# The running state of a scan mixer formed and kept transposed, and turned back once a tile

## The reference

```
alpha = exp(dt_t * A_neg);  beta = (1 - lam_t) * dt_t * alpha;  gamma = lam_t * dt_t
Bx_t  = u_t[:, :, :, None] * Bp_t[:, :, None, :]
h     = alpha * h + beta * Bx_prev + gamma * Bx_t
y_t   = einsum('bhpn,bhn->bhp', h, Cp_t)
```

## Time and profile before

| | |
|---|---|
| median of 3 runs | 4490.3 us (4488.98 to 4494.2) |
| the profiled execution: its time, its span | 4485.84 us, 4484.1 us |
| third stage in the trace | about 240 to 3266 us |
| TensorE (PE) busy over the span | 4197.9 us, 94% |
| VectorE, ScalarE, GpSimd busy | 3222.6 us (72%), 2157.4 us (48%), 2376.0 us (53%) |

### The profile page before, as it was taken

How to read it: one execution, slowest core, us unless ns; L and a number is a source line. 1 busy time by engine, 2 the same in 40 slices (tenths; PEclk the granted TensorE clock), 3 DMA queues, 4 the chain that set the end, 5 groups by cost and what they waited for, 6 DMA issues and landing times. The chain is left out here.

```text
span 4484.1 us, 118726 instructions
## 1 busy us (share of the span) xinstructions
PE 4197.9 (94%) x39924; PEld 3488.0 (78%) x39924; DVE 3222.6 (72%) x6737; ACT 2157.4 (48%) x5046; POOL 2376.0 (53%) x3284
## 2 busy tenths in 40 slices
PE   5389999999999999999999999999869999989999
PEld 3178788888888888878788788888648888878888
DVE  8867777777677776777767777677636666668888
ACT  3234444454444444444444444444446666645555
POOL 3276666666676666766666666666400000026666
PEclk9699999999999999999999999999979999989999
DMA  8321111111111111111111111111056666633333
GB/s 276 117 81 30 48 39 39 47 39 48 36 38 50 39 48 36 39 50 39 39 45 39 50 39 36 48 39 46 23 134 180 188 180 183 186 94 105 105 105 96
DMA packets 369774, 347.50 MB, mean 77 GB/s; under 512 B 24953, under 2 KB 343289, under 8 KB 360185
## 3 DMA queue, kind: packets, MB, share of 16 engines
q1 hardware_dynamic: 352380, 323.98, 24.2%
q10 hardware_dynamic: 16896, 16.78, 1.1%
HBM read 232.01 MB, written 108.66 MB: 76 GB/s over the span
## 5 line engine op out<-in xcount | busy, mean ns | idle before, releaser
L721 PE MATMUL bank<-w_bc,xnT 128*128 128x512 f32 x3072 | 804.3, 404 | 11.7 <-POOL xnT L1042 11.7
L924 ACT COPY turned_t<-bank 128x512 f32<-128x512 f32 x512 | 300.3, 587 | 982.4 <-PE bank L744 982.3
L721 PEld LDWEIGHTS bank<-w_bc,xnT 128*128 128x128 f32 x3072 | 556.8, 189 | 144.7 <-issue 34.5
L1455 PE MATMUL p_yc<-sig,toep 64*64 64x256 f32 (+14 forms) x16384 | 538.1, 282 | 13.7 <-issue 10.5
L1455 PEld LDWEIGHTS p_yc<-sig,toep 64*64 64x64 f32 x16384 | 475.1, 132 | 89.7 <-issue 43.5
L1050 POOL TENSOR_TENSOR steps<-upto,par 128x512 fp32r<-128x512 f32 x512 | 536.6, 1068 | 0.0
L1159 DVE TENSOR_TENSOR rot<-bank,par 128x512 f32<-128x512 f32 x512 | 350.1, 684 | 209.6 <-PE bank L721 124.7
L1059 POOL TENSOR_TENSOR turned_b<-rot 128x512 f32<-128x512 f32 x256 | 325.9, 1273 | 197.7 <-DVE rot L1160 197.5
L1604 POOL MEMSET xT<- 128x258 f32 x1 | 0.3, 314 | 684.2 <-POOLq L1349 684.2
L1059 POOL TENSOR_TENSOR turned_c<-rot 128x512 f32<-128x512 f32 x256 | 354.5, 1385 | 1.8 <-DVE rot L1160 1.8
L1160 DVE TENSOR_TENSOR rot<-bank,par 128x512 f32<-128x512 f32 x512 | 346.9, 677 | 0.0
(11 more groups left out here) (264 smaller groups left out, 9671.5 us busy)
## 6 DMA issues: line engine op xcount, KB each, us to landing
toep<-taps_dram SPq DMA_DIRECT2D x256, 260.0 KB, 4.1
el<-el_dram SPq DMA_DIRECT2D x256, 128.0 KB, 3.0
xg<-arg_x SPq DMA_DIRECT2D x32, 512.0 KB, 5.1
xnT_dram<-xt_g ACTq DMA_DIRECT2D x32, 512.0 KB, 5.4
xnT_raw<-xnT_dram SPq DMA_DIRECT2D x128, 128.0 KB, 2.5
x_quad<-arg_x SPq DMA_DIRECT2D x32, 512.0 KB, 3.9
x_dram<-x_quad SPq DMA_DIRECT2D x32, 512.0 KB, 3.7
x0T_dram<-conv SPq DMA_DIRECT2D x32, 512.0 KB, 2.8
```

The source lines that it names most:

```text
L721: last = mm(p_bc[c][:, :], xnT[w.q % 2][p][:, k, :], w_bc[q][:, k, c * 1024 + g * W4:c * 1024 + (g + 1) * W4], start=(n == 0), stop=(n == ...
L924: s_.copy(turned_t[g][c][:, :], p_tr[:, :]).then_inc(s[f"copy_{BC[c]}"], 1)
L1455: last = mm(by_seq(p_y[p][c][odd * H:(odd + 1) * H, 0:2 * TILES])[:, :, first:], toep[n % SLOTS][c * H:(c + 1) * H, lag * H:(lag + 1) * H] ...
```

## The change

The state is kept a second time, in `state_p`, with 64 head columns on partitions: the even heads on partitions 0 to 63, the odd ones on 64 to 127, and for each pair of heads 128 state columns along, again 128 x 512. `new_state` now takes `u_w` of a head as the stationary operand (128 x 64) and B (128 x 128) as the moving one, and writes 64 partitions. `fade_state` and `carry_state` work on `state_p`. A new step of TensorE, `turn_state`, transposes it in four 128 x 128 pieces into the bank of the transposes, and a new step of ScalarE, `copy_state`, copies that to `state`, which `outputs` reads as before. The decay over a tile is the same on all partitions, so that 4 columns of scalars hold what 8 did, one half of the partitions for even and one for odd heads.

```
-P_COS, ... P_EL, P_ET, P_ALL = 0, 8, 24, 40, 48, 56, 64, 72, 80
+P_COS, ... P_EL, P_ET, P_ALL = 0, 8, 24, 40, 48, 56, 64, 72, 76
...
-            s_.activation(col(P_ET), as3(pp[2][:, :]), ACT.Exp)
+            for e in range(2):
+                rows = slice(e * HEAD_U, (e + 1) * HEAD_U)
+                s_.activation(params[rows, :, P_ET:P_ET + HEADS // 2], as3(pp[2][rows, :])[:, :, e::2], ACT.Exp)
...
-    BANK_TR = (..., ("over_b0", "copy_b0", 1, 0))
+    BANK_TR = (..., ("over_b0", "copy_b0", 1, 0), ("turn_state", "copy_state", 1, -1))
...
             def outputs(i, w, g):
-                wait_for(pe, "carry_state", i - 1)
+                wait_for(pe, "copy_state", i - 1)
...
             def new_state(i, w):
                 for h in range(HEADS):
-                    v = slice(h * HEAD_U, (h + 1) * HEAD_U)
-                    last = mm(p_state[:, v], turned(w, h // GROUP, 0)[:, (h % GROUP) * STATE:(h % GROUP + 1) * STATE], u_w[:, v],
-                              start=True, stop=True)
+                    pair, e = h // 2, h % 2
+                    last = mm(p_state[e * 64:(e + 1) * 64, pair * STATE:(pair + 1) * STATE], u_w[:, h * HEAD_U:(h + 1) * HEAD_U],
+                              turned(w, h // GROUP, 0)[:, (h % GROUP) * STATE:(h % GROUP + 1) * STATE], start=True, stop=True)
...
+            def turn_state(i, w):
+                wait_for(pe, "carry_state", i)
+                bank_read(pe, BANK_TR, "turn_state", i + 1)
+                for pair in range(4):
+                    c = slice(pair * 128, (pair + 1) * 128)
+                    last = tp(p_tr[:, c], state_p[1 - w.q % 2][:, c], ident[:, :])
+                last.then_inc(s["turn_state"], 1)
...
                     tile(q, 0, project_u)
+                    tile(q, 1, turn_state)
                     if q == 1:
                         quad(2, widen, 4)
...
+            def copy_state(i, w):
+                wait_for(act, "turn_state", i)
+                wait_for(act, "outputs1", i - 1)
+                s_.copy(state[1 - w.q % 2][:, :], p_tr[:, :]).then_inc(s["copy_state"], 1)
...
                     tile(q, 0, copy_turned, 0, 0)
+                    tile(q, 1, copy_state)
                     if q == 0:
                         quad(2, normalised, 2, 1)
...
             for p in range(2):
                 g_.memset(state[p][:, :], 0.0)
+                g_.memset(state_p[p][:, :], 0.0)
...
             def fade_state(i, w):
                 wait_for(pool, "carry_state", i - 1)
-                wait_for(pool, "outputs1", i - 1)
-                g_.tensor_tensor(all_heads(state[1 - w.q % 2][:, :]), all_heads(state[w.q % 2][:, :]), over(param(P_ET, w), HEAD_U),
+                wait_for(pool, "turn_state", i - 2)
+                g_.tensor_tensor(heads(state_p[1 - w.q % 2][:, :]), heads(state_p[w.q % 2][:, :]), over(par[w.p][:, w.q, P_ET:P_ET + HEADS // 2], STATE),
                                  ALU.mult).then_inc(s["fade"], 1)
...
             def carry_state(i, w):
-                v_.tensor_tensor(state[1 - w.q % 2][:, :], p_state[:, :], state[1 - w.q % 2][:, :], ALU.add)
+                v_.tensor_tensor(state_p[1 - w.q % 2][:, :], p_state[:, :], state_p[1 - w.q % 2][:, :], ALU.add)
```

More of the change, by code:

```diff
@@ L22 @@
 LN_EPS, RMS_EPS = 1e-5, 1e-6
-P_COS, P_SIN, P_A, P_G, P_RHO, P_W, P_EL, P_ET, P_ALL = 0, 8, 24, 40, 48, 56, 64, 72, 80
+P_COS, P_SIN, P_A, P_G, P_RHO, P_W, P_EL, P_ET, P_ALL = 0, 8, 24, 40, 48, 56, 64, 72, 76
 P_EARLY = P_G
@@ L549, in mixer_and_first_ffn @@
     decay, own, mix = two("decay", [128, W4]), two("own", [128, W4]), two("mix", [128, W4])
-    u_g, u_w, state = sb("u_g", [128, 512]), sb("u_w", [128, 512]), two("state", [128, 512])
+    u_g, u_w, state, state_p = sb("u_g", [128, 512]), sb("u_w", [128, 512]), two("state", [128, 512]), two("state_p", [128, 512])
     y_from, yT, el = two("y_from", [128, H64]), two("yT", [128, 512]), two("el", [128, 4, TOK])
@@ L567, in mixer_and_first_ffn @@
     names = ("project_b project_c rotate_b rotate_c turn_b turn_c over_b over_c copy_b copy_c steps logs exp diagonal own gram mix outputs take_y "
-             "values gate_values weigh_values new_state fade carry_state split_hi split_rest sum_over mean_sq square_y pair_sums scan_rstd project_out "
+             "values gate_values weigh_values new_state fade carry_state turn_state copy_state split_hi split_rest sum_over mean_sq square_y pair_sums scan_rstd project_out "
              "residual1 rstd1 norm1 xn_over first_column shifted mixed key relu key_sq receptance tanh value gated residual2 rstd2 norm2 "
@@ L590, in wait_loaded @@
         wait(eng, s[f"{what}{w.p}"], 16 * ((w.n - w.p) // 2 + 1) if isinstance(w.n, int) else 8 * (w.n + (2 - w.p)))
-    BANK_TR = (("over_c1", "copy_c1", 1, -1), ("over_b1", "copy_b1", 1, -1), ("over_c0", "copy_c0", 1, 0), ("over_b0", "copy_b0", 1, 0))
+    BANK_TR = (("over_c1", "copy_c1", 1, -1), ("over_b1", "copy_b1", 1, -1), ("over_c0", "copy_c0", 1, 0), ("over_b0", "copy_b0", 1, 0), ("turn_state", "copy_state", 1, -1))
     BANK_ARG = (("logs0", "exp0", 1, 0), ("new_state", "carry_state", 1, -1), ("logs1", "exp1", 1, 0))
@@ L1193, in carry_state @@
                 wait_for(dve, "new_state", i)
-                v_.tensor_tensor(state[1 - w.q % 2][:, :], p_state[:, :], state[1 - w.q % 2][:, :], ALU.add).then_inc(s["carry_state"], 1)
+                v_.tensor_tensor(state_p[1 - w.q % 2][:, :], p_state[:, :], state_p[1 - w.q % 2][:, :], ALU.add).then_inc(s["carry_state"], 1)
             def moments(which, places, src, by):
```

## The result

The changed kernel takes 4518.7 us (median of 5 runs, 4514.18 to 4520.99), the one before 4490.25 in the same session (4488.98 to 4494.2): 1.006 times as long, interval 1.0045 to 1.0074. It is slower by 28 us, outside my range. The profiled execution took 4520.99 us, its span is 4519.3.

A forecast was written before the change was run, and what follows sets the result against it. TensorE bounds three quarters of the tiles, a chain outside it q = 0. A quad: +0.56 + d - 0.35 - 0.26 = -0.08 us, times 31 -2.5; +1.05 for zeroings; in all -1.4, giving 4489 us, range 4470 to 4505.

The forecast's parts named there:

- q = 0: Tile ending on a chain outside TensorE: TensorE's gain lost, the copy ahead of `xn` costs 0.56 us a quad, plus d.
- TensorE's sum: `new_state` 0.70 us less, `turn_state` 0.35 or 0.44 more; 1.31 us a quad, 41 us; as a rival, whole: 4450, chance 0.11.
- q = 2: Tile where ScalarE is free and the copy lies under `key` 1: TensorE gains 0.26 us.
- q = 3: Tile where TensorE gains 0.35 us, if anyone uses it; the copy makes `split_xnT` and `y_sq` up to 0.25 late.
- q = 1: Tile where TensorE gains 0.35 us and the copy delays four activations about 1 us, costed at nothing.
- the cover: In q = 1, ScalarE's 1.51 us idle ahead of the next `copy_turned` takes up the copy's 1 us delay.
- d: Move of VectorE's full stretch ahead of the carry in q = 0: between -0.35 and +0.25 or +0.4 us, taken as -0.03.
- hurt twice: Rival: late `y_sq` makes `y_sum` overlap `cut_decay`, 0.72 for 0.46 us; a quad loses 0.35; 4502, chance 0.15.
- the first rival: Chain moves up with TensorE as overlap of `steps` and `cut_decay` resolves: d -0.35, a quad gains 0.40; 4479, chance 0.22.
- the rival's 4502: Time in us of the rival where the copy's late `y_sq` also slows `y_sum`; d about +0.4, chance 0.15.
- The missing overlap: Rival: the pair's heads don't overlap, `new_state` stays near 1.73 us; 1.7 us a quad, 4544, chance 0.05.

The follow-up runs named there:

- packed_only: Changed kernel without `turn_state` and `copy_state`, leaving out the part of y from the state before the tile; 4442.1 us, 0.989 of the kernel before.
- late_copy: Changed kernel with `copy_state` moved behind ScalarE's work for the quads, in q = 3 left in place; 4504.3 us, 1.0027 of the kernel before.
- next_tile: Changed kernel with `turn_state` and `copy_state` moved into the next tile, behind `project_bc` and `square_y`; 4488.9 us, 0.9994 of the kernel before.
- lean_before: Kernel before, with one wait for each PSUM bank use, for the use just before; 4442.2 us, 0.989 of the kernel before.
- lean_after: Changed kernel with one wait for each PSUM bank use, for the use just before; 4454.6 us, 0.9915 of the kernel before.
- next_tile_lean: `next_tile` with one wait for each PSUM bank use; 4428.1 us, 0.986 of the kernel before.
- same_waits: Changed kernel, `turn_state` waiting only for the bank use before it and old uses, except the first, not for `copy_state`; 4513.0 us, 1.0046.
- behind_after: Changed kernel with single waits only in `turn_over` 0,1 and `project_out`, the two steps behind `new_state`; 4515.2 us, 1.0053 of the kernel before.
- turn_only: Kernel before, with four transposes of `state` and a copy to an unread tile at the places of the change; 4565.5 us, 1.0163.

## Why the prediction was wrong

The medians over the quads, from one start to the next (`x2n_over` stands at the end of q = 0; us):

```
                  last new_state   to new_   to new_    to new_    to new_    quad
                  to x2n_over      state 1   state 2    state 3    state 0
before                 8.37         15.98     23.68      28.11      17.77     93.95
after                  9.10         16.05     23.55      28.33      17.65     94.75
packed_only            8.29         16.08     23.07      27.74      17.20     92.46
late_copy              8.62         16.05     23.54      28.39      17.64     94.28
next_tile              7.85         16.52     23.57      28.19      17.64     93.78
lean_before            8.37         15.27     23.01      27.89      17.78     92.32
lean_after             9.10         15.37     22.85      27.74      17.65     92.73
next_tile_lean         7.83         15.81     22.86      27.73      17.65     91.88
```

**What failed is "TensorE's sum"**: that TensorE alone gains 0.35, 0.35, 0.26 and 0.35 us. I had priced each group by the distance from its start to the next, and the groups beside it at nothing. Measured against that, a quad has 1.13 us that were in none of those distances: 0.56 at the edges of the packed form, 0.18 behind `turn_state`, 0.33 by waits of the queue, and 0.06 for `turn_state` in q = 0. TensorE's waits in q = 0 came out 0.25 smaller than said. What is left, 0.88 us a quad or 27 us, is the whole way from -0.08 to +0.80.

*The edge of the packed form.* The group in front of `new_state` costs 0.09 us more in every tile, the one behind 0.05, with or without the waits: 0.56 us a quad, 17 us in all. I could have read it. A `gram` ahead of the packed `outputs` and one ahead of `turn_over`, in the kernel before:

```profile
1005.11 1.05 PE L754 MATMUL bank<-turned_t 128*128 128x128 f32 x8
1006.09 0.44 PE L772 MATMUL bank<-mix,u_g 128*64 128x128 f32 x4
```

```profile
1046.96 1.06 PE L754 MATMUL bank<-turned_t 128*128 128x128 f32 x8
1047.86 0.60 PE L744 MATMUL bank<-ident,turned_c 128*128 128x128 f32 x4
```

The same eight matmuls take 0.98 us to the next start ahead of the 64-column form and 0.90 ahead of the 128-column one. The load rows above fit that: the load of `new_state` no longer runs ahead of its matmul. Why it doesn't is not shown.

*Behind the transposes.* In the same way a rounded group behind `turn_state` costs 0.09 more (`widen`, `decay_logs`), 6 us; I had taken `turn_state` ahead of a rounded matmul from a place whose follower's own price I didn't look at.

*The waits of the queue.* They cost 16 us more in the changed kernel. About 6 are the waits that the change adds (`same_waits`), 3.5 to 7 those behind the shorter `new_state` (`behind_after`). These may overlap in part, and how the rest splits, behind `turn_state` in q = 2 and in its row of waits, is open. In the distances, 0.80 us a quad between the two kernels have become 0.41 between the lean ones; of these 0.39 us (12 of the 16), 0.08 are found at `turn_over` in q = 2, 0.10 at `project_out`, 0.08 at `turn_state` in q = 2 and 0.07 at `key`.

**q = 0: right.** From `new_state` of q = 3 by way of `new_state` 0 to `x2n_over` I had +0.53, the trace has +0.61. The carry is where it was, `turn_state` waits for it, the copy is in front of `xn`. In the kernel before, `x2n_over` starts 2.57 us behind the carry (the medians of the table under q = 3 below), in the change 3.06: 0.49 for the copy, where I had 0.56. In `late_copy` and `next_tile` it is 2.57 and 2.56 again. So `x2n_over` hangs on VectorE's chain in all of them, and the wait of `turn_state` for the carry by itself makes `x2n_over` no later. `next_tile` gave more than `late_copy` because the chain starts earlier there (below). In the count of TensorE's waits I had said 1.23 us and found 0.98.

**q = 1: the cover held.** ScalarE, here with the copy ahead of the four activations, then with the next `copy_turned`:

```profile
1097.35 0.59 ACT L940 COPY state<-bank 128x512 f32<-128x512 f32 x1 [1.24 <-PE bank L791]
1097.83 2.09 ACT L956 ACTIVATE xn<-x_quad,shift,rstd 128x256 f32<-128x256 f32 x4
...
1104.73 0.59 ACT L935 COPY turned_t<-bank 128x512 f32<-128x512 f32 x1 [0.69 <-PE bank L746]
```

Of its 1.51 us of idle time, 0.69 are left, and TensorE does not wait there. But the sum over this tile's groups fell by 0.09 us and not by 0.35: the edge in front, 0.05 behind, `widen` 0.09, `project_out`.

**q = 2** lost 0.18 us where I said a gain of 0.26: the 0.44 are the edges, the waits behind `new_state` and at `turn_state`, which came at 0.51 for 0.44, and `key`.

**q = 3 and d.** `new_state` 3 to `new_state` 0 is 0.12 shorter, `steps` is still 2.49 us long, and `y_sum` took 0.46 us in the quad shown, so the copy didn't hurt twice. d, by the carry, is +0.11 for my -0.03. I had the copy ahead of `split_xnT` (L914), the head of the chain, and that later by up to 0.25; it is 0.17. What I had wrong is why the chain doesn't move up: I put TensorE's gain in q = 3 down as one that nobody uses. `split_xnT` waited for TensorE's `project_u` before, and now stands behind the copy:

```profile
1148.14 0.59 ACT L940 COPY state<-bank 128x512 f32<-128x512 f32 x1 [1.24 <-PE bank L791]
1148.62 0.41 ACT L914 CAST xnT<-xnT_raw 128x256 fp32r<-128x256 f32 x1
```

From the start of `new_state` of q = 3 to the starts of the chain's steps (median over 26 quads, us):

```
                split_xnT    y_sq    carry   x2n_over
before             7.20      8.08    23.58     26.15
after              7.37      8.16    23.69     26.75
turn_only          8.04      8.84    24.35     27.41
packed_only        6.52      7.40    22.93     25.50
late_copy          7.37      8.16    23.69     26.26
next_tile          6.52      7.40    22.92     25.48
```

In all six the carry comes 15.5 us behind `y_sq`: the chain moves as one piece, with `steps` at 2.49 us in `packed_only` too. Without transposes and copy ahead of `split_xnT` it starts 0.68 us earlier, about what the shorter `new_state` of q = 3 gives (0.70 less 0.05 behind it). In the change the transposes and the copy use all of that up, and `late_copy` leaves the copy there. So TensorE's gain in q = 3 does count, and the first rival didn't need the overlap of `steps` and `cut_decay` to resolve; it needed the two new steps out of the way. That is what `next_tile` has over `late_copy`: 0.78 us up to `x2n_over`, of which the transposes take back 0.47 in the tile behind it; 0.20 more lie in q = 2.

The 4518 us lie above the rival's 4502, but not by its mechanism.

**The missing overlap** is refuted by 1.03 us in each of the four tiles. The Trainium skill's rule ("TensorE: Matmul & The Clock Gate", Part 3, The mechanism) would have given near 1.73 there. It doesn't explain the edge of the group either: before the change `new_state` has all 128 rows too, and its first load runs 0.24 us ahead of its matmul, while the group in front still runs.

## What to carry to other kernels

On an engine that is nearly always busy, price a new form of a group together with both neighbours, from a place in the trace where that form already stands behind and ahead of the same kind of group: four edges of 0.14 us ate a fifth of the gain here. Put a step that needs a late result where that result has long been there, not where it is first possible, and don't let it stand in an engine's queue ahead of the first step of a chain: the same transposes and copy cost 30 us less one tile later. And before shortening matmuls, count the waits on their queue; a wait that an earlier step has already made is the cheapest thing to remove.

## What was not expected of the hardware

TensorE's queue is slow at waits that are already fulfilled. In q = 2 of the changed kernel they stand in a row (TensorE's queue, between 1113.45 and 1115 us):

```profile
L38 PEldq EVENT_SEMAPHORE  x13: 51/51/51, 1113.5 to 1114.9; - x13
```

Each is shown with 51 ns, but thirteen start over 1.4 us, about 0.11 us apart. As long as the queue is ahead of the matmuls they cost nothing, and most do: removing 5891 from the kernel before saved 50 us, 8 ns each. The price comes where a long row meets a short group: `sum_over` took 0.55 us with them and 0.14 without.
